# Writing out the image loop of a two-block attention and spectral kernel, and moving its side work to other steps

## The reference, cut to what matters

```
x = x + attention(groupnorm(x))      # 12 heads of 16, softmax over 1024 tokens, then w_o
x = x + spectral(groupnorm(x))       # below

def spectral(x, w1, b1, w2, b2, bias_w, bias_b):
    bias = x @ bias_w.T + bias_b
    xf = rfftn(x in 4 blocks of 48 channels, axes=(1, 2), norm='ortho')
    r1 = relu(mul(xr, w1[0]) - mul(xi, w1[1]) + b1[0]);  i1 = relu(mul(xr, w1[1]) + mul(xi, w1[0]) + b1[1])
    r2 = mul(r1, w2[0]) - mul(i1, w2[1]) + b2[0];        i2 = mul(r2, w2[1]) + mul(i1, w2[0]) + b2[1]
    return irfftn(complex(r2, i2), norm='ortho') + bias
```

## Time and profile before

| what | value |
|---|---|
| time, median of 3 runs | 1609.42 us (1605.87 to 1610.75) |
| time of the profiled execution | 1600.23 us |
| its span | 1598.4 us |
| granted TensorE clock over the span | 0.954 |
| PE busy | 1487.2 us (93%) |
| DVE busy | 1166.4 us (73%) |
| ACT busy | 1006.8 us (63%) |
| POOL busy | 189.6 us (12%) |
| DMA of instructions | 175 packets, 2.20 MB |

### The profile page before, as it was taken

How to read it: one execution, slowest core, us unless ns; L and a number is a source line. 1 busy time by engine, 2 the same in 40 slices (tenths; PEclk the granted TensorE clock), 3 DMA queues, 4 the chain that set the end, 5 groups by cost and what they waited for, 6 DMA issues and landing times.

```text
span 1598.4 us, 31556 instructions
## 1 busy us (share of the span) xinstructions
PE 1487.2 (93%) x9972; PEld 720.6 (45%) x9972; DVE 1166.4 (73%) x2153; ACT 1006.8 (63%) x2017; POOL 189.6 (12%) x277
## 2 busy tenths in 40 slices
PE   6799989999999999999899998999999999999766
PEld 4344433545444544545444453445544453434244
DVE  3787877887798777897599775987799778884131
ACT  1065776667767775677567675667777677667312
POOL 2000000030014000030011200140010300030000
PEclk9697998999999998999899998999999999999989
DMA  5320213223432333233332323323332323321213
GB/s 129 61 49 25 59 42 69 42 74 70 83 85 67 78 70 67 59 84 70 74 81 58 77 73 65 80 60 78 69 82 56 78 62 68 66 61 43 75 27 82
DMA packets 101167, 107.64 MB, mean 67 GB/s; under 512 B 25152, under 2 KB 77824, under 8 KB 100992
## 3 DMA queue, kind: packets, MB, share of 16 engines
q1 hardware_dynamic: 100992, 105.44, 29.5%
HBM read 27.51 MB, written 6.68 MB: 21 GB/s over the span
## 4 chain that ended last, share of the span: by engine, by line
PE 69%; issue 11%; DVE 10%; DMA 3%; POOL 3%; SPq 2%; ACT 1%; DVEq 0%; POOLq 0%; ACTq 0%
PE o_acc L1269 18%; PE scores L1216 13%; PE ring L1248 12%; PE ring L1292 9%; DVE row_max L1024 7%; PE ring L1401 2%; PE ring L1281 2%; PE ring L1388 2%; PE ring L1394 2%; PE ring L1380 2%; PE ring L1311 1%; DMA inv_all<-inv_rows 1%; PE scores L1292 1%; PE ring L1303 1%; PE ring L1407 1%
## 5 line engine op out<-in xcount | busy, mean ns | idle before, releaser
L1024 DVE TENSOR_REDUCE row_max<-ring 128x1 f32<-128x512 f32 x1536 | 968.6, 680 | 219.4 <-PE ring L1248 214.1
L932 ACT ACTIVATE probs<-scores 128x512 f32<-128x512 f32 x1536 | 822.7, 599 | 253.3 <-PE scores L1216 249.6
L1248 PE MATMUL ring<-k_stack,q_stack 48*128 48x512 f32 x1536 | 595.7, 470 | 25.0 <-DVE row_max L1024 20.8
L1216 PE MATMUL scores<-q_stack,k_stack 50*128 50x512 f32 x1536 | 602.6, 468 | 3.8 <-DMA q_stack<-shift 2.5
L1269 PE MATMUL o_acc<-probs,v_aug 128*18 128x512 f32 x3072 | 418.2, 617 | 2.8 <-ACT probs L932 1.8
L1216 PEld LDWEIGHTS scores<-q_stack,k_stack 50*128 50x128 f32 x1536 | 252.0, 189 | 295.4 <-ACT probs L932 250.5
L1248 PEld LDWEIGHTS ring<-k_stack,q_stack 48*128 48x128 f32 x1536 | 255.5, 191 | 147.9 <-DVE row_max L1024 105.1
L573 POOL TENSOR_TENSOR inv_all<-o_raw,inv_all 128x1024 f32<-128x1024 f32 x23 | 54.8, 2381 | 697.7 <-DMA inv_all<-inv_rows 697.7
L1269 PEld LDWEIGHTS o_acc<-probs,v_aug 128*18 128x18 f32 x3072 | 52.0, 96 | 121.7 <-issue 77.5
L1096 DVE TENSOR_TENSOR x<-ring,x 128x192 f32<-128x192 f32 x62 | 19.3, 352 | 63.7 <-PE ring L1292 63.6
L1292 PE MATMUL ring<-xt,w_qk 64*128 64x256 f32 x504 | 62.9, 384 | 0.1
(11 more groups left out here) (152 smaller groups left out, 1129.1 us busy)
## 6 DMA issues: line engine op xcount, KB each, us to landing
q_stack<-qk_parts SPq DMA_DIRECT2D x288, 64.0 KB, 2.2
k_stack<-qk_parts SPq DMA_DIRECT2D x144, 128.0 KB, 4.2
inv_all<-inv_rows SPq DMA_DIRECT2D x24, 512.0 KB
rows_b<-rows_a SPq DMA_DIRECT2D x128, 96.0 KB, 2.8
spec_b<-spec_a SPq DMA_DIRECT2D x64, 102.0 KB, 2.4
x_in<-in_x_dram SPq DMA_DIRECT2D x8, 768.0 KB, 10.4
x_res<-in_x_dram SPq DMA_DIRECT2D x8, 768.0 KB, 5.7
o_t<-inv_all SPq DMA_DIRECT2D x192, 32.0 KB, 1.9
```

The source lines that it names most:

```text
L932: nc.scalar.activation(probs[:, GH * (s % 2) + h, :], scores[:, n % SCORE_BANKS, :], ACT.Exp, scale=SCALE).then_inc(probs_made, 1)
L1024: nc.vector.tensor_reduce(row_max[:, which, m:m + 1], max_bank(g, unit, i), AX.X, ALU.max).then_inc(max_taken, 1)
L1216: mm(scores[:, n % SCORE_BANKS, :], k_stack[rows, 2 * g + hp, P * kt:P * (kt + 1)], q_stack[rows, g, half, hp, :], start=True, stop=True). ...
L1248: mm(max_bank(g, unit, i), q_stack[rows, g, half, hp, P * qt:P * (qt + 1)], k_stack[rows, 2 * g + hp, HALF * which:HALF * (which + 1)], st ...
```

## The change

The loop is gone: bodies 1 to 6 are called one after another, so that all eight are straight code on every engine, with constants in place of registers. Beside it the tables are new. Most pieces that stood in the middle of a step stand at the head of one now, pieces are moved by a step or a few, the token operations, the follow-up work of DVE, the stacking DMAs and five single placements change. No operation is added or removed.

```diff
 PREP_AT
-    18: ([('qk', 2)], []),
-    26: ([('qk', 3)], []),
-    28: ([('qk', 4)], []),
-    32: ([('qk', 5)], []),
-    34: ([('v', 0)], []),
+    19: ([('qk', 2)], []),
+    23: ([('qk', 3)], []),
+    27: ([('qk', 4)], []),
+    32: ([('qk', 5)], [('v', 0)]),
     37: ([], [('v', 1)]),
-    44: ([('v', 2)], []),
-    45: ([('v', 3)], [])}
+    39: ([('v', 2)], []),
+    47: ([('v', 3)], [])}
 POST_AT
-    13: ([('proj', 3)], [('turn', 0)]),
-    14: ([], [('turn', 1)]),
-    15: ([('turn', 2)], []),
-    17: ([], [('mean', 0)]),
+    13: ([('proj', 3)], []),
+    14: ([('turn', 0)], []),
+    15: ([('turn', 1)], []),
+    16: ([('turn', 2)], []),
+    18: ([('mean', 0)], []),
     19: ([], [('var', 0)]),
-    21: ([], [('spread', 0)]),
-    25: ([('dftw', 0)], [('dftw', 1)]),
-    27: ([('dftw', 2)], []),
-    28: ([], [('dftw', 3)]),
+    22: ([('spread', 0)], []),
+    25: ([('dftw', 0)], []),
+    26: ([('dftw', 1)], []),
+    27: ([], [('dftw', 2)]),
+    28: ([('dftw', 3)], []),
...
-    38: ([('mix1', 5), ('mix1', 6), ('mix1', 7)], []),
-    39: ([('lin', 2)], []),
+    37: ([('mix1', 2)], []),
+    38: ([('mix1', 3), ('mix1', 4), ('mix1', 5), ('mix1', 6), ('mix1', 7)], []),
...
-    46: ([('idfth', 0)], [('idfth', 1), ('idfth', 2)]),
-    47: ([('idfth', 3)], []),
-    48: ([('lin', 3)], []),
-    53: ([], [('idftw', 0)]),
-    55: ([('idftw', 1)], [('idftw', 2)]),
-    56: ([('idftw', 3)], [])}
+    44: ([('lin', 2)], []),
+    45: ([('idfth', 0), ('idfth', 1), ('idfth', 2)], []),
+    46: ([('idfth', 3)], []),
+    50: ([('lin', 3)], []),
+    53: ([('idftw', 0)], []),
+    54: ([], [('idftw', 1)]),
+    55: ([('idftw', 2)], [('idftw', 3)])}
-PREP_FOLLOW = {0: [('stats', 0), ('stats', 1)], 3: [('stats', 2)], 6: [('gather', 0)], ...}
-POST_FOLLOW = {13: [('stats', 0)], 14: [('stats', 1)], 16: [('stats', 2), ('gather', 0)], 20: [('normalise', 0)], 22: [('normalise', 1)], 24: [('normalise', 2)]}
-PLACE_V_AT = {24: 2, 44: 0, 47: 1}
-TOKENS_AT = {20: (0,), 23: (1,), 24: (2,), 25: (3,), 26: (4,), 29: (5,)}
-STACK_AT = {10: 'q0', 11: 'q1', 14: 'k'}
+PREP_FOLLOW = {0: [('stats', 0)], 3: [('stats', 1)], 6: [('stats', 2)], 7: [('gather', 0)], ...}
+POST_FOLLOW = {14: [('stats', 0)], 15: [('stats', 1)], 16: [('stats', 2), ('gather', 0)], 26: [('normalise', 0), ('normalise', 1)], 27: [('normalise', 2)]}
+PLACE_V_AT = {26: 2, 40: 0, 45: 1}
+TOKENS_AT = {20: (0,), 21: (1,), 24: (2,), 27: (3,), 28: (4,), 30: (5,)}
+STACK_AT = {10: 'q1', 11: 'q0', 13: 'k'}
-SPREAD_AT = 2
+SPREAD_AT = 5
-RESIDUAL_AT = 16
-LOAD_AT = 5
+RESIDUAL_AT = 17
+LOAD_AT = 3
@@ batches
             body(0, True, False)
-            body(1, True, True)
-            with eng.Fori(2, NB - 2) as b:
+            for b in range(1, NB - 1):
                 body(b, True, True)
-            body(NB - 2, True, True)
             body(NB - 1, False, True)
```

More of the change, by code:

```diff
@@ L66 @@
     12: ([('proj', 2)], []),
-    13: ([('proj', 3)], [('turn', 0)]),
-    14: ([], [('turn', 1)]),
-    15: ([('turn', 2)], []),
-    17: ([], [('mean', 0)]),
-    19: ([], [('var', 0)]),
-    21: ([], [('spread', 0)]),
-    25: ([('dftw', 0)], [('dftw', 1)]),
-    27: ([('dftw', 2)], []),
-    28: ([], [('dftw', 3)]),
-    29: ([('lin', 0)], []),
[L77 to L81, removed]
@@ L82 @@
-    36: ([('lin', 1)], []),
-    37: ([('mix1', 3), ('mix1', 4)], []),
-    38: ([('mix1', 5), ('mix1', 6), ('mix1', 7)], []),
-    39: ([('lin', 2)], []),
-    40: ([('mix2', 0)], []),
-    41: ([('mix2', 1), ('mix2', 2)], [('mix2', 3)]),
-    42: ([('mix2', 4)], []),
-    46: ([('idfth', 0)], [('idfth', 1), ('idfth', 2)]),
-    47: ([('idfth', 3)], []),
-    48: ([('lin', 3)], []),
-    53: ([], [('idftw', 0)]),
-    55: ([('idftw', 1)], [('idftw', 2)]),
-    56: ([('idftw', 3)], [])}
-PREP_FOLLOW = {0: [('stats', 0), ('stats', 1)], 3: [('stats', 2)], 6: [('gather', 0)], 12: [('normalise', 0)], 13: [('normalise', 1)], 14: [('normalise', 2)]}
@@ new lines @@
+    25: ([('dftw', 0)], []),
+    26: ([('dftw', 1)], []),
+    27: ([], [('dftw', 2)]),
+    28: ([('dftw', 3)], []),
+    29: ([('lin', 0)], []),
+    30: ([], [('dfth', 0), ('dfth', 1)]),
+    31: ([('dfth', 2)], []),
+    33: ([('dfth', 3), ('dfth', 4), ('dfth', 5)], []),
+    34: ([('mix1', 0)], []),
+    35: ([('mix1', 1)], []),
+    36: ([('lin', 1)], []),
+    37: ([('mix1', 2)], []),
+    38: ([('mix1', 3), ('mix1', 4), ('mix1', 5), ('mix1', 6), ('mix1', 7)], []),
+    40: ([('mix2', 0), ('mix2', 1)], []),
@@ new lines @@
+    41: ([('mix2', 2), ('mix2', 3)], []),
+    42: ([('mix2', 4)], []),
+    44: ([('lin', 2)], []),
[5 more added lines that the diff above has]
+    55: ([('idftw', 2)], [('idftw', 3)])}
+PREP_FOLLOW = {0: [('stats', 0)], 3: [('stats', 1)], 6: [('stats', 2)], 7: [('gather', 0)], 12: [('normalise', 0)], 13: [('normalise', 1)], 14: [('normalise', 2)]}
+POST_FOLLOW = {14: [('stats', 0)], 15: [('stats', 1)], 16: [('stats', 2), ('gather', 0)], 26: [('normalise', 0), ('normalise', 1)], 27: [('normalise', 2)]}
```

## The result

The changed kernel takes 1520.31 us (median of 4 runs, 1516.42 to 1528.75) against 1608.51 for the kernel before on the same chip: a ratio of 0.9459, 95% interval 0.9417 to 0.9502. It is faster by 88 us, where 52 were forecast; the time lies under the range of 1540 to 1579. The profiled execution is the slowest of the four, 1528.75 us with a span of 1527.0.

The account below looks back on a forecast made before the run. PE, busy 93% of the span, was taken as the bound, through its waits and clock. Terms -31 - 5 - 20 + 6 - 2 = -52 us from 1600.2 gave 1548, plus 9 to the median: 1557 us, range 1540 to 1579.

Parts of the forecast that it names:

- Branches back, 31: Ends of images 2, 3 and 4: idle time and half clock at each loop branch go, 10.4 us each, 31 saved.
- Registers, 5: Loop body: register instructions working out wait counts go, 1.1 us for each of four images plus entry and exit, 5 saved.
- The rival that straight code can't be fetched: All image borders: fetching written-out code stops PE at each of seven, 73 us paid, 1630 us in all; chance 0.04.
- dftw 0, 20: Around step 25: moving qk 2 and qk 3 removes PE's waits and the slow stretches behind them, 20 us saved.
- Spread behind the load, +6: Images 2 to 5: load issued before spread delays proj 0 by 1.0 us each, plus one 3.4 us slow stretch.
- Image 1: Image 1: maxima in time at step 8, but proj 0 waits; 7.2 us lost now against some 5, gain 2.
- Moves with one answer, nothing: Stack order, regrouping of the mixed spectrum for idfth, and START for MID: priced at no gain and no cost.
- START for MID (the same products before and after): Pieces moved from the middle of a step to its head: priced at nothing.
- The sum, 1548: All terms, -52 us, taken from the earlier kernel's profiled execution of 1600.2 us, before adding 9 for the median.

Follow-up runs that it names:

- old_qk: straight_old with qk 2 moved from step 18 to 19 and qk 3 from step 26 to 23; 1547.07 us, ratio 0.9622 to the kernel before.
- straight_old: The kernel before with its old tables, the loop replaced by all images written out; 1568.05 us, ratio 0.9788 to the kernel before.
- second profile: The changed kernel run and profiled again without edits, beside others on one chip; 1520.89 us, ratio 0.9465 to the kernel before.
- new_mid: The changed kernel with sixteen pieces moved from a step's head to the middle of a step, mostly the step before; 1553.88 us, ratio 0.9695.
- spread_first: The changed kernel with the spread at step 2 instead of 5 and the image load at step 5 instead of 3; 1513.64 us, ratio 0.9447.
- old_head2: old_qk with eleven pieces moved from the middle of a step to a head that comes in time; 1538.54 us, ratio 0.9601.

## Why the prediction was off

**Branches back, 31: right.** At the borders they cost 31.5 us with the old tables (10.2, 10.6 and 10.7), of which a few tenths are registers, and 26 with the new. **Registers, 5: about right.** 1.0 to 1.1 us per image with the old tables in 35 of 48 steps, so some 1.5 for all of them (an estimate), for 1.1 forecast; about half of that with the new. The whole of the loop is 34 to 43 by the runs, against 36.

The Trainium skill's "Advanced Engine Details and Errata", section "Control Flow Timing", gives a compare-and-branch about 108 ns. Here one taken branch back of this loop cost 10 to 11 us with the old tables and 8 to 9 with the new, far above that figure. The Trainium skill's "Runtime: NRT & Kernel Launch", section "Instruction fetch mechanics", says that a taken branch to a block that is not on hand forces a fetch. The trace agrees: idle time in front of whatever piece stands first, and three packets of q8 within 10 us at each branch back. Straight code of eight images moved less over the instruction queues than the loop did. The rival that straight code can't be fetched is refuted.

**dftw 0, 20: right.** By the runs old_qk stands 21 to 27 us under straight_old. In the profiles images 1 to 6 are 28.6 us shorter, and 5.0 of this are the maxima of image 1. Steps 22 to 25 give 20.3 us against the kernel before, of which about 2 come back in steps 26 to 31. In the changed kernel only 0.29 us in image 2 stayed.

**Spread behind the load, +6: right.** Waits of 1.04, 0.43, 1.52 and 0.85 in images 2 to 5 for the 1.0 forecast; the slow stretch did not come, so 4 (5 in the second profile). **Image 1:** proj 0 waits 2.63 us for about 3 forecast; the image gains 7.7 in all, with its share of dftw 0.

**"Moves with one answer, nothing": this step failed.** It held "START for MID (the same products before and after)" and gave it no cost, since the products are the same. new_mid shows that the place has a price: sixteen pieces, 5.0 us per image. Image 6, straight code in both kernels, shows what the tables gave here. Before it took 176.1, of which 2.9 were idle and 3 were lost to a slow stretch, so 170.2 without the stall; old_qk, the old tables without the stall, has 171.1. After it takes 167.3. That is 2.9 to 3.8 us in an image with the same instructions, 17 to 23 for images 1 to 6. (Steps 27 to 46 of the earlier trace rows can't be used for it: after, they hold 12 products fewer.) I had looked only for idle time of PE between products, and this loss shows as none.

Between stall-free images 4 under the old and the new tables (171.6 in old_qk, 168.1 in spread_first) lie 3.5 us. Eleven moves to a head give 1.7. The other 1.8 were not traced to an entry; 1.4 of them lie in steps 26 to 43. By new_mid's 0.3 us the 15 moves to a head less the four to the middle would be 3.4, but old_head2 got half of that price for its eleven, so the agreement may be chance. How the place of a piece comes to cost time stays open.

**The other half of the miss is the step from profile to median.** The sum, 1548, was 19.3 us above the profiled execution, 1528.75. I then added 9 since the profiled run of before lay 9 under its median; that of after lies 8.4 over its own. A difference of one execution was carried over as if it belonged to the kernel: 17.4 of the 36.7 us by which the forecast missed. The terms that came out right are right against profiles, not against medians.

## What to carry to other kernels

Where three engines hand tiles round in a fixed order, don't price a move within a step at nothing because the work is the same: try it. Here the head of a step was better than its middle by 0.3 us on the average of sixteen pieces, and for some by nothing. Before moving a piece later, follow every queue its result passes: a variance half a step later fell behind a waiting multiply on POOL and left PE idle for 7 to 9 us in each image, and transfers issued a little later fell behind others that SP was waiting to issue. A range needs the scatter of single executions in it when the sum is made against one profile.

## What was not expected

- PE can lose time and read as fully busy: old_qk is busy for 171.14 of 171.63 us in image 4 and spread_first for 167.89 of 168.13, both at full clock and with the same 1232 products. Counted from start to start, most of the difference stands in front of the pieces' own products.
- The length of a wait alone does not tell whether the lower clock follows: behind one of 1.18 us in image 3 of straight_old it does (granted clock 0.75 as a mean from 689.7 to 696.5), behind the 1.52 us of proj 0 in image 4 of the changed kernel it does not. In the kernel before the same holds: the prediction says that a slow stretch follows every wait but the shortest, but behind the 2.31 us of dftw 0 in image 2 the clock stayed at 1.00.
- The instruction queues moved more with the loop (2.20 MB) than without it (1.75).
